# A transformer layer on one core: GpSimd splits w1's first block alone, transposes wait for halves of a tile, and three pieces of the order move at the end of attention

## What is computed

```python
x = x + attention(layernorm(x))       # rms norm, 16 heads of 64, softmax, w_out
x = x + ffn(layernorm(x))
# attention: sim = (q * 64**-0.5) @ k.T ; attn = softmax(sim) ; out = (attn @ v) @ w_out
# ffn: (gelu(x @ w1 + b1) @ w2 + b2) * sum of the two largest router shares, made to sum to 1
```

## Time and profile before

| | |
|---|---|
| median of three runs | 1212.01 us (1211.71 to 1213.29) |
| the profiled execution, its time | 1211.5 us |
| its span in the trace | 1209.7 us |
| mean granted clock of TensorE | 0.998 of full speed |
| TensorE busy | 1189.3 us (98%) |
| its weight loads | 1040.2 us (86%) |
| Vector busy | 964.9 us (80%) |
| Scalar busy | 890.3 us (74%) |
| GpSimd busy | 641.4 us (53%) |

### The profile page before, as it was taken

The page is one execution under the profiler, slowest core; times in us unless marked ns, Lnnn a source line. Parts: engine busy times, 40 slices in busy tenths (PEclk is TensorE's granted clock), DMA queues, the critical chain, the costliest instruction groups (busy, mean ns, idle before and its releaser), DMA issues. The chain is left out here.

```text
span 1209.7 us, 29228 instructions
## 1 busy us (share of the span) xinstructions
PE 1189.3 (98%) x11351; PEld 1040.2 (86%) x11351; DVE 964.9 (80%) x1746; ACT 890.3 (74%) x1922; POOL 641.4 (53%) x800
## 2 busy tenths in 40 slices
PE   8999999999999999999999999999999989999998
PEld 6778888888888888888888888888888878888887
DVE  5788888888888888888888888889888987666644
ACT  6888788878888888888878887888888884334332
POOL 5665556555655565555555655556555664222221
PEclk9999999999999999999999999999999999999999
DMA  5122111311131113111311131113111232111100
GB/s 159 36 56 69 36 36 37 88 37 36 37 88 36 36 37 88 36 37 37 88 36 36 37 88 37 36 36 88 36 36 37 71 89 74 36 57 49 35 19 35
DMA packets 33464, 62.91 MB, mean 52 GB/s; under 512 B 5808, under 2 KB 9904, under 8 KB 33328
## 3 DMA queue, kind: packets, MB, share of 16 engines
q1 hardware_dynamic: 33328, 61.05, 19.7%
HBM read 19.08 MB, written 8.39 MB: 23 GB/s over the span
## 5 line engine op out<-in xcount | busy, mean ns | idle before, releaser
L876 POOL TENSOR_SCALAR prob<-prob,rowinv 128x512 f32<-128x512 f32 x512 | 350.2, 699 | 312.3 <-DVE rowinv L1063 311.2
L786 ACT ACTIVATE prob<-ps,negmax 128x512 f32<-128x512 f32 x512 | 347.1, 686 | 35.7 <-DVE negmax L1058 31.9
L982 DVE TENSOR_TENSOR pT_lo<-ps,pT_hi 128x512 fp32r<-128x512 f32 (+1 forms) x384 | 320.2, 861 | 25.9 <-ACT pT_hi L777 19.6
L1058 DVE TENSOR_REDUCE negmax<-ps 128x2 f32<-128x1024 f32 x256 | 310.8, 1215 | 0.7 <-PE ps L503 0.6
L530 PEld LDWEIGHTS ps<-identity,prob 64*128 64x128 f32 x4096 | 154.6, 139 | 64.7 <-issue 35.8
L774 ACT ACTIVATE pT_hi<-ps 128x1024 fp32r<-128x1024 f32 x128 | 131.5, 1027 | 101.1 <-issue 100.3
L530 PE MATMUL ps<-identity,prob 64*128 64x64 f32 x4096 | 177.4, 226 | 8.8 <-POOL prob L876 3.6
L499 PE MATMUL ps<-nat 64*128 64x512 f32 x1024 | 173.3, 415 | 2.2 <-ACT prob L786 1.0
L544 PE MATMUL ps<-pT_hi,vbuf 128*128 128x256 f32 x1024 | 164.4, 283 | 2.9 <-DVE pT_lo L982 2.9
L544 PE MATMUL ps<-pT_lo,vbuf 128*128 128x256 f32 x1024 | 164.0, 282 | 0.0
L544 PEld LDWEIGHTS ps<-pT_hi,vbuf 128*128 128x128 f32 x1024 | 144.2, 190 | 9.8 <-DVE pT_lo L982 4.2
(11 more groups left out here) (121 smaller groups left out, 2317.0 us busy)
## 6 DMA issues: line engine op xcount, KB each, us to landing
att_hi_v<-halves_out SPq DMA_DIRECT2D x128, 128.0 KB, 2.3
att_lo_v<-halves_out SPq DMA_DIRECT2D x128, 128.0 KB, 2.4
xres<-in_x SPq DMA_DIRECT2D x8, 512.0 KB, 3.5
x_scratch<-xres SPq DMA_DIRECT2D x8, 512.0 KB, 2.9
out_y<-f_o SPq DMA_DIRECT2D x16, 256.0 KB, 2.0
xin<-in_x SPq DMA_DIRECT2D x7, 512.0 KB, 4.3
wstage<-in_w SPq DMA_DIRECT2D x4, 512.0 KB, 3.8
xin<-x_scratch SPq DMA_DIRECT2D x3, 512.0 KB, 3.7
```

The lines of the kernel that those rows point to most:

```text
L786: act.activation(prob[:, n % NPROB, j * SEQ:(j + 1) * SEQ], ps[:, PS_SCORE[n % 2] + j, :], ACT.Exp, bias=negmax[:, n % 4, j:j + 1], accum_ ...
L876: return pool.tensor_scalar(dst, src, scalar, 1.0, ALU.mult, ALU.mult)
L982: return dve.tensor_tensor(dst, full, hi, ALU.subtract)
L1058: dve.tensor_reduce(negmax[:, n % 4, :], ps[:, PS_SCORE[n % 2]:PS_SCORE[n % 2] + 2, :], AX.X, ALU.max, negate=True).then_inc(s_max, 1)
```

## The change

Four edits:

1. Chunk 8 (the first half of w1) is rounded and subtracted by GpSimd, one slot earlier (249), behind the normalisation of tile 248 and behind a wait for the last k product. Scalar and Vector skip it. Its position in the table of slots also lets SP issue the load of chunk 9 earlier.
2. `transpose_prob` waits for the first head's probabilities before its first transpose and for the second head's before its ninth. The wait for the probabilities now stands behind the others.
3. In steps 127 and 128, Vector does the output add ahead of the reciprocal of an odd tile.
4. In step 129, TensorE does the fourth up block ahead of the last PV instead of behind the output block.

```diff
-        POOL_CHUNKS = (0, 1, 2, 3, 4, 5, 6, 7)
+        POOL_CHUNKS = (0, 1, 2, 3, 4, 5, 6, 7, 8)
+        POOL_HI = (8,)
...
-        slot_of_chunks.update({NUNIT - 6: [8], NUNIT - 4: [9], NUNIT: [10], NUNIT + 2: [11]})
+        slot_of_chunks.update({NUNIT - 7: [8], NUNIT - 4: [9], NUNIT: [10], NUNIT + 2: [11]})
...
             def transpose_prob(n):
 
-                pe.wait_ge(s_prob, 2 * n + 2)
...
                 for a in range(2 * TT):
+                    if a % TT == 0:
+                        pe.wait_ge(s_prob, 2 * n + a // TT + 1)
                     for r in range(2):
...
                 if 0 <= tail < TAIL_UPS:
                     up(0, tail)
+                if step == LAST_STEP:
+                    up(0, tail + 1)
                 if 0 <= step - 2 < STEPS:
                     weighted_values(step - 2)
                 for block_of_aux in rest:
                     aux(step, *block_of_aux)
-                if 0 <= tail < TAIL_UPS:
+                if 0 <= tail < TAIL_UPS and step < LAST_STEP:
                     up(0, tail + 1)
...
                 for i in weight_slots(slot):
+                    if i in POOL_HI:
+                        continue
                     wait_weight_loaded(act, i)
...
                         if i in POOL_CHUNKS:
+                            hi_part, lo_part = weight_chunk(i)[1]
+                            if i in POOL_HI:
+                                wait_weight_loaded(pool, i)
+                                pool.wait_ge(s_auxfull, aux_index[("k", NPAIR - 1)] + 1)
+                                times(hi_part, weight_stage(i), 1.0).then_inc(s_whi, 1)
                             pool.wait_ge(s_whi, i + 1)
-                            hi_part, lo_part = weight_chunk(i)[1]
...
             for step in range(FIRST_STEP, LAST_STEP + 2):
-                if 0 <= 2 * step - 1 < NUNIT:
+                if 0 <= 2 * step - 1 < NUNIT and step < STEPS - 1:
                     row_inverse(2 * step - 1)
                 for block_of_aux in late_blocks(step - 1):
                     if block_of_aux[1] < 4:
                         aux_done(*block_of_aux)
+                if 0 <= 2 * step - 1 < NUNIT and step >= STEPS - 1:
+                    row_inverse(2 * step - 1)
```

## The result

| | before | after |
|---|---|---|
| median of six runs on one chip | 1212.12 us | 1206.55 us (1206.26 to 1208.19) |
| the profiled execution | 1211.5 | 1207.04 |
| its span | 1209.7 | 1205.2 |

The ratio is 0.9955, with a 95% interval from 0.9944 to 0.9965: 5.6 us faster (4.2 to 6.8), where the forecast had 2.9 and the range ended at 1207.9. Profiled execution against profiled execution it is 4.5, which lies inside the interval. What follows accounts for the 4.5; the 1.1 between the two figures is in no trace.

A forecast was written before the change was run, and what follows sets the result against it. TensorE, busy 1189.3 of 1209.7 us, was taken as the bound, so only waits could be won: 1.3 + 0.7 + 0.9 = 2.9 us, giving a median of 1209.1; range over all 1207.9 to 1211.2.

The forecast's parts named there:

- Halves of a tile: Transposes: the first eight of a late tile run while GpSimd makes the second half; 1.3 us won.
- upper bound of 1.5: Late transpose tiles: four big ones win 0.25 each, five small ones 0.5 together; 1.5 us at most.
- cap of 0.25 per tile: Late transpose tiles: eight transposes are issued in 0.25 us, so a big late tile ends 0.25 earlier.
- lower end of "nothing": Late transpose tiles: no gain if the engines behind are not ready and the wait reappears.
- w1's first block: Around tile 249: without Scalar's rounding of this block, its transposes and the following scores come 0.7 us earlier.
- the 974.5: Sign at tile 249: GpSimd's two new instructions would end before 974.5 us.
- GpSimd is late: Rival at tile 249: GpSimd's new instructions take over 5 us, losing the 0.7; 1209.8 to 1210.5, chance 0.05.
- Output adds before reciprocals: Steps 127 and 128: tile 254 is issued 0.8 us earlier; part of the tail's 0.9 in all.
- Fourth up block: Before the last PV: six matmuls fill 0.6 us of waiting; part of the tail's 0.9 in all.
- what is late next is Vector's chain: After the change, Vector's hidden low parts, normalisation and adds would be the next thing late.
- Vector's chain is no bound: Rival: Vector moves earlier with TensorE, tail wins 1.4 and halved waits 1.5; 3.6 us, 1208.4, chance 0.13.
- Given back: Rival: late tiles gain nothing, the tail only 0.4; 1.3 us in all, 1210.7, chance 0.28.

The follow-up runs named there:

- before_again: The kernel before, unchanged, profiled a second time; one run, 1212.98 us.
- before_shift16: The kernel before with 16 wide warming matmuls at the start replaced by 64 narrow ones, 96 more TensorE instructions; 1.0047 of before.
- chunk8: The kernel before with only the change's first edit, w1's first half rounded and subtracted by GpSimd; 0.9997 of before.
- adds_up: The kernel before with only the third and fourth edits, the earlier output adds and the earlier fourth up block; 0.9993 of before.
- halves: The kernel before with only the second edit, a probabilities wait per half tile, behind the tile's other waits; 0.9972 of before.
- after_early: The changed kernel with the first three of Vector's last four output adds ahead of its part of the eighth hidden block; 1207.58 us, 0.9944 of before.
- waitlast: The kernel before with the whole tile's wait for probabilities moved behind the other waits, not halved; 1.0006 of before.
- normfirst: The kernel before with GpSimd normalising the even tile ahead of the regrouped attention output instead of behind it; 1.0000 of before.

## Why the prediction was right or wrong

**Halves of a tile** is the term that failed: 1.3 was written, the body gained 2.7 in the two profiles shown. By several runs it is 3.1: the five bodies with the old wait (before, before_again, before_shift16, chunk8, adds_up) have a mean of 917.1, halves, after and after_early one of 914.0. Two steps of its working were wrong.

First, the upper bound of 1.5 was worked out from the nine late tiles of one trace and taken as a property of the kernel. The other traces with the old wait show up to 4.2 us of lateness in the body. With the same cap of 0.25 per tile chunk8 gives 2.3 where the first gave 1.5 (tile 2 in both). On average these five had 2.9 of lateness in the body, and halves, after and after_early 1.0: 1.9 of the 3.1. Pauses of about 0.3 stay in the middle of late tiles, as the cap says.

Second, the edit also puts the wait for the probabilities behind the others, and the working gave that no price; the tiles in time were put at nothing or a loss. They gain 1.0 us over the 120 even tiles of the body, and waitlast, which halves nothing, has the same gain in them. The 0.2 that are left are no more than these bodies differ among themselves.

The lower end of "nothing" and the upper end of 1.5 both left that out, so the range ended at 1207.9, above the median. That the fast end was missed by 1.35 us is not all shown: by the traces the terms are 3.1, 0.85 and 0.65, together 4.6, and the median moved by 5.6.

In a tile in time the wait is met: the ninth load starts 0.06 ahead of its matmul like its neighbours, and nothing is lost; the measurement decides.

**w1's first block**: 0.7 forecast, 0.82 at tile 249, 0.85 in the tail of chunk8. GpSimd ended both at 970.88, well before the 974.5, since the rounding took 1.04 instead of 1.36, and since tile 248 was 2.9 earlier by then (in before's time they end at 973.8). "GpSimd is late" fell.

**Output adds before reciprocals** and **Fourth up block**: 0.9 forecast, 0.65 alone (adds_up) and as much in the full change beyond chunk8 and halves. From tile 249 to tile 254 TensorE won 1.0, where 0.8 was forecast; the up block fills the 0.6 us wait in front of the last PV. At the last transposes ahead of the first down block TensorE had won 2.3 since tile 248, at that block 1.75, at the end 1.57. So 0.56 is given back in front of the block, where the prediction had 0.5, and for the reason it gave, that "what is late next is Vector's chain". The new wait row names the output adds. Another 0.18 goes behind the block, which the prediction did not have. "Vector's chain is no bound" fell here: after_early, which loosens that chain, gains 0.8 more.

**Given back** fell: the late tiles did gain, and the tail won 1.57 where this rival had 1.1.

That the tail came out at 1.6 as forecast is partly luck: w1's block gave 0.15 more than its 0.7, and the other term 0.25 less than its 0.9.

## What to carry to other kernels

A wait that is short and rare in one profile is a sample: before pricing its removal, find what makes it late, and take the sum from more than one trace or from all places that it can strike. When an edit moves a wait as well as splitting it, price the move by itself: the order of waits decides which of them rides on the load. Halving a wait caps such a delay; moving work that waits for a DMA behind work that others need takes it away, provided that nothing then meets it on a shared port. When a reorder shows the expected waits gone and no gain, look at the small instructions of the engine beside it.

## What the runs showed of the hardware

- **Instruction packets delay data.** 91 packets of 16 KB come in 1.2 ms; in the kernel before, a regrouping of four transfers of 128 KB that meets one within the first 3.5 us lands 0.8 to 1.9 us later. With ninety-six more instructions on TensorE other pairs were late, 13 of 15.
- **A small Vector instruction can take GpSimd's time.** A `TENSOR_SCALAR` of 128x4 took 1.29 us beside GpSimd's add of 1.29 (normfirst, eight of eight), 0.16 in the kernel before.
- **A wait that is met costs nothing on a weight load**, even in a stream whose matmuls start every 0.03 us: 256 of them, and the time went down.
- **A wait that ends late costs more as an instruction of its own.** The first transpose follows the end of GpSimd's work by 0.147 us when the wait stands ahead of the load (waitlast, 13 tiles), by 0.055 when it rides on it (before, 8 tiles).
